# Attention scores as one product of 128 rows per head, with the rope addition split into two halves on GpSimd

## The chip, the cores and the metric

The kernel is one program on one core of a Trainium2 chip. TensorE (PE) multiplies, VectorE (DVE), ScalarE (ACT) and GpSimd (POOL) do the elementwise work, and SyncE (SP) issues the DMAs. The metric is the device time of one execution in microseconds, the lower the better; of several runs the median is given.

## The reference

Two adaLN layers over x of 4 x 512 tokens x 256. The change touches only the attention of the second layer. What it computes there, per batch entry b (4 of them, 512 tokens, 16 query heads, 4 key groups):

```python
qkv = hidden_states @ Wqkv
q, c_kv = jnp.split(qkv, [NH * D_QK], axis=-1)        # c_kv: a latent of 64 per token
q = q.reshape(b, s, NH, D_QK)                         # D_QK = 128 (nope) + 64 (rope)
k = (c_kv @ Wk_up).reshape(b, s, NKV, D_QK)
v = (c_kv @ Wv_up).reshape(b, s, NKV, D_V)
q = jnp.concatenate([q_nope, _rope(q_rope, s)], axis=-1)
k = jnp.concatenate([k_nope, _rope(k_rope, s)], axis=-1)
scores = jnp.einsum('bqhd,bkhd->bhqk', q, k) * scale  # k repeated for 4 heads each
scores = jnp.where(causal[None, None], scores, jnp.finfo(scores.dtype).min)
probs = jax.nn.softmax(scores, axis=-1)
out = jnp.einsum('bhqk,bkhd->bqhd', probs, v).reshape(b, s, NH * D_V)
return out @ Wo
```

`_rope(x)` is `x * cos + rot * sin`, with `rot` the two halves of the 64 rope rows swapped, one of them negated.

## The kernel before

The first layer (a recurrent attention with Newton-Schulz steps, then a feed-forward part) runs up to about 575 us; the second layer's attention runs from 575 to 1018 us; a mixture of experts ends the kernel.

The attention works in the latent space: the nope part of a key is the 64-row latent `ckvT` itself, because the key weights were multiplied into the query weights beforehand (`w_abs`). So a score is a sum over 128 numbers per head: 64 of the query's latent against `ckvT`, and 64 of the roped query against the roped key. Before, they are two products of 64 rows each that add up in one PSUM bank (L2098 and L2101). `q_latent` and `q_rope` hold two heads stacked: head e of a pair in rows 64e to 64e+63. `ckvT` and `keys` hold the same 64 rows twice, so that either head finds them in its own rows. The four products of a pair of heads are a *block*: latent e=0, latent e=1, rope e=0, rope e=1. All are f32, and an f32 product shows in the trace as two weight loads and two passes (MATMUL records), so a block has eight passes.

Work goes in 16 *batches*, each a tile of 128 query rows of one b, in the order q = 1, 3, 0, 2 (`ORDER`), so that the keys seen are 256, 512, 128 and 384 columns wide (causal). I number them n = 0 to 15. A batch has 8 *slots* of a pair of heads each; slot t = 8n + p. In slot t the order written out by hand for each engine is:

- PE: `score(t + 2)`, a block (two slots ahead of the softmax), and then what `Plan` puts into the slot: parts of `weigh(n - 1)` (probabilities by values, products of 32 rows, L2118, at p = 2 and 3, in two parts, or in one where n % 4 is 3), `project_out(n - 1)` (L2132, 8 passes of 256 columns each at p = 6 and 7), `project_q` for the rope rows of the next batch (p = 0, 1) and for its latent rows (p = 4, 5, or 3, 4 where n % 4 is 3), each 16 passes of 128 columns at L2056; the next b's values (L2064) and keys (L2073, a product of 64 rows), and the transposes of a norm (L1591).
- DVE: `largest(t)` (L2454, masks the scores and takes the row maximum, twice), `turn(t - 2)` (L2468, transposes in blocks of 32), `invert(t)` (L2473), and then rotations of queries (L2479) and keys (L2483, L2484), `gate_out`, norms.
- ACT: `exponential(t)` (L2354, twice), `take_out` (L2363), and the copies out of PSUM, `take_rope` (L2342), `take_latent` (L2346), `take_ckv` (L1979), `take_key` (L2334).
- POOL: `add_rope` due for the slot (L2693 multiplies the swapped rows by sin, L2696 adds them to the rows times cos and writes `q_rope`; half 0 and half 1 of the next batch, ahead of `normalize` in slots p = 5 and 6), `add_key` (L2701), `normalize(t)` (L2707), `add_out` (L2714).
- SP: `swap_rope`, `swap_key` (L2779), four DMAs each, and `spread_key` (L2793), four DMAs of 128 KB that write a group's roped key into both row halves of `keys`.

The waits that matter here: `score(t)` waits for the two maxima of slot t - 2, whose banks it takes; at p = 0 and p = 4 it waits for `taken` of the latent half and for `q_roped` of the rope half; at the first batch of a b it waits for `ckv_taken` and for `keys_spread`. `turn(t - 2)` waits for `normalize(t - 2)`. `project_q` waits until ACT has taken what stood in its bank.

Of the kernel before, what the change touches and what calls it, by code (L numbers as in the profile page):

```python
# [1826 lines left out]
def stage_rest(k):  # L1827
# [34 lines left out]
    q_latent, q_rope = (k.wq_switch[:, 2 * NP * P * n:2 * NP * P * (n + 1)].rearrange("p (f n c) -> p f n c", f=2, n=NP) for n in range(2))  # L1862
# [19 lines left out]
    spare = q_rope[:, 0].rearrange("p n c -> p (n c)")  # L1882
    gt, eq = (spare[:, B * E * E * n:B * E * E * (n + 1)].rearrange("p (b e f) -> p b e f", b=B, e=E) for n in range(2))
    bd = [spare[:, 512 + 256 * w:768 + 256 * w].rearrange("p (c b s f) -> p c b s f", c=2, b=B, s=S2) for w in range(2)]
    spare = q_latent[:, 0].rearrange("p n c -> p (n c)")
# [36 lines left out]
    MOVE = 16 * 4  # L1922
# [62 lines left out]
    with nc.Block() as block:  # L1985
        @block.tensor
        def _(pe):
# [93 lines left out]
            def score(t):  # L2081
# [6 lines left out]
                if p % HP == 0:  # L2088
                    wait_taken(pe, "latent", n, p // HP)
                    pe.wait_ge(s["q_roped"], 2 * n + p // HP + 1)  # L2090
                    if n % QT == 0:
                        pe.wait_ge(s["ckv_taken"], 2 * (b + 1))
                        pe.wait_ge(keys_spread[p // HP], MOVE * (b + 1))
                halves = [slice(LORA * e, LORA * e + LORA) for e in range(2)]
                for e, rows in enumerate(halves):
                    if t >= AHEAD:
                        pe.wait_ge(s["maxed"], 2 * (t - AHEAD) + e + 1)
                    nc.tensor.matmul(score_bank[t % AHEAD][e][:, 0:width(n)], q_latent[rows, n % 2, p, :],  # L2098
                                     ckvT[rows, b % 2, 0:width(n)], start=True, stop=False)
                for e, rows in enumerate(halves):  # L2100
                    nc.tensor.matmul(score_bank[t % AHEAD][e][:, 0:width(n)], q_rope[rows, n % 2, p, :],  # L2101
                                     keys[b % 2][rows, p // 2, 0:width(n)], start=False, stop=True).then_inc(s["scored"], 1)
# [214 lines left out]
        def _(act):  # L2317
# [12 lines left out]
            def take_key(b, f):  # L2330
                wait_made(act, "key", b, f)
                if b > 0:
                    act.wait_ge(keys_spread[f], MOVE * b)
                nc.scalar.activation(key_x[b][:, f], filled("key", b, f)[:], ACT.Copy).then_inc(taken_of("key", b, f), 1)  # L2334

            def take_rope(n, half):
                wait_made(act, "rope", n, half)
                if n > 0:
                    act.wait_ge(s["q_roped"], 2 * (n - 1) + half + 1)
# [4 lines left out]
            def take_latent(n, half):  # L2344
                wait_made(act, "latent", n, half)
                nc.scalar.activation(q_latent[:, n % 2, HP * half:HP * half + HP, :].rearrange("p n c -> p (n c)"),  # L2346
                                     filled("latent", n, half)[:], ACT.Copy).then_inc(taken_of("latent", n, half), 1)
# [85 lines left out]
        def _(dve):  # L2433
# [24 lines left out]
            def turn(t):  # L2458
# [6 lines left out]
                if p == 0 and n % QT == 0:  # L2465
                    for f in range(2):
                        dve.wait_ge(keys_spread[f], MOVE * (n // QT + 1))
# [465 lines left out]
```

## Time and profile before

| | |
|---|---|
| median of 3 runs | 1076.84 us (1074.63 to 1078.26) |
| the profiled execution | 1076.94 us |
| its span, first to last instruction | 1075.1 us |
| mean granted TensorE clock | 0.992 of full speed |
| PE busy | 1016.1 us, 95% |
| DVE, ACT, POOL busy | 703.8, 546.1, 433.7 us |
| block products L2098 and L2101, PE busy | 105.8 and 93.5 us (47.5 + 46.0) |
| rope addition L2696 on POOL | 39.2 us in 30, and two more at the start |

The busy time of an engine counts overlapping instructions once. A matmul's record runs until its last result is out, so two passes overlap; what a pass costs PE is read from start to start. In a timeline row the first number is the start, the second the time to the last end, then engine, line, operation, tiles, shape and count; in brackets stands the idle time ahead of it and what ended it.

### The profile page before, as it was taken

Reading aid. Unit: us, or ns where it says so; the run is one execution under the profiler, and the core shown is the slowest. Engines: PE = TensorE matmul, PEld = TensorE weight load, DVE = VectorE, ACT = ScalarE, POOL = GpSimd, SP = SyncE. Lnnn points to the kernel's source line nnn. Section 1 sums busy time; section 2 is a strip of 40 time slices with the busy share of each in tenths; the row PEclk is TensorE's granted clock in tenths of the full one; section 3 lists DMA queues with packets and bytes.
Section 4 is the critical chain, followed back from the end, with each engine's and each line's share of the span. In section 5 each row is a group of like instructions: output and inputs, shape, how many; then the busy total and the mean of one; then the engine's idle time right before and its main releaser. Section 6 shows DMA issues by size and latency. Waiting matters only on the chain.

```text
span 1075.1 us, 25979 instructions
## 1 busy us (share of the span) xinstructions
PE 1016.1 (95%) x10226; PEld 739.7 (69%) x10226; DVE 703.8 (65%) x2121; ACT 546.1 (51%) x1418; POOL 433.7 (40%) x391
## 2 busy tenths in 40 slices
PE   6788999999999999999999999999999999999978
PEld 4567888888878546655667576766767686758646
DVE  4888898898899713122225675747584767667774
ACT  2667777777778531212132543545454545444441
POOL 1222033134145411010106474747475756778610
PEclk9999999999999999999999899999999999999999
DMA  9150000000000009100013011200120003000202
GB/s 322 44 185 2 1 0 0 0 0 0 1 2 2 1 1 294 46 1 1 1 30 70 15 27 31 64 7 21 36 65 22 21 22 79 22 21 22 80 2 80
DMA packets 27887, 44.03 MB, mean 41 GB/s; under 512 B 6928, under 2 KB 16912, under 8 KB 26896
## 3 DMA queue, kind: packets, MB, share of 16 engines
q1 hardware_dynamic: 27792, 42.71, 13.5%
q8 instruction: 66, 1.08, 0.4%
q14 instruction: 29, 0.24, 0.1%
HBM read 21.98 MB, written 2.10 MB: 22 GB/s over the span
## 4 chain that ended last, share of the span: by engine, by line
PE 53%; DVE 5%; ACT 2%; issue 1%; POOL 0%; DVEq 0%
PE quad L2056 10%; PE quad L1705 8%; PE quad L2098 7%; PE quad L2118 7%; PE quad L2101 6%; PE quad L2000 5%; PE quad L2132 5%; PE quad L2196 1%; PE quad L2064 1%; ACT act_probs L2354 1%; PE quad L1591 1%; DVE act_probs L2454 1%; ACT act_probs L2363 1%; PE quad L2019 1%; DVE x_pairs L2484 1%
## 5 line engine op out<-in xcount | busy, mean ns | idle before, releaser
L2707 POOL TENSOR_TENSOR act_probs<-act_probs,rden 128x512 f32<-128x512 f32 (+3 forms) x128 | 171.0, 1339 | 155.7 <-DVE rden L2473 155.6
L2354 ACT ACTIVATE act_probs<-act_probs,neg_max 128x256 f32<-128x256 f32 (+3 forms) x256 | 140.8, 552 | 82.9 <-DVE neg_max L2454 82.6
L2056 PEld LDWEIGHTS quad<-hT,ug_queries 128*128 128x128 f32 x1024 | 120.5, 194 | 30.6 <-issue 18.6
L2056 PE MATMUL quad<-hT,ug_queries 128*128 128x128 f32 x1024 | 132.2, 283 | 3.0 <-ACT act_probs L2363 2.2
L2454 DVE CUSTOM_DVE_ANT_0 act_probs<-quad,mask 128x256 f32<-128x256 f32 (+3 forms) x256 | 115.1, 486 | 6.8 <-PE quad L2101 6.1
L1705 PE MATMUL quad<-hT,ug_raw_switch 128*128 128x512 f32 x256 | 115.8, 602 | 0.0
L2098 PE MATMUL quad<-ckvT,ug_raw_switch 64*128 64x512 f32 (+3 forms) x512 | 105.8, 480 | 6.9 <-DVE neg_max L2454 6.9
L2473 DVE RECIPROCAL rden<-den 128x2 f32<-128x2 f32 x128 | 20.6, 161 | 120.2 <-ACT act_probs L2354 120.1
L1720 DVE SCALAR_TENSOR_TENSOR act_probs<-quad,ws_up,silu_keys 128x512 f32<-128x512 f32 x32 | 24.0, 750 | 102.4 <-ACT silu_keys L1715 102.4
L1705 PEld LDWEIGHTS quad<-hT,ug_raw_switch 128*128 128x128 f32 x256 | 48.0, 192 | 55.7 <-issue 55.5
L1715 ACT ACTIVATE silu_keys<-quad,ws_gate 128x512 f32<-128x512 f32 x32 | 22.0, 687 | 120.5 <-PE quad L1705 120.5
L2468 DVE STREAM_TRANSPOSE wq_wo<-act_probs 128x1024 f32<-128x1024 f32 (+1 forms) x64 | 70.8, 1106 | 3.1 <-POOL act_probs L2707 3.1
L2098 PEld LDWEIGHTS quad<-ckvT,ug_raw_switch 64*128 64x128 f32 x512 | 41.7, 186 | 39.8 <-issue 20.6
L2132 PE MATMUL quad<-down_keys,act_probs 128*128 128x256 f32 x256 | 63.5, 392 | 0.8 <-ACT act_probs L2363 0.8
L1426 POOL TENSOR_TENSOR hidden<-gate_silu,hb 128x256 f32<-128x256 f32 x16 | 12.0, 753 | 124.5 <-ACT hb L969 124.5
L2132 PEld LDWEIGHTS quad<-down_keys,act_probs 128*128 128x128 f32 x256 | 46.1, 189 | 19.2 <-issue 11.4
L2000 PE MATMUL quad<-down_raw_out,act_probs 128*128 128x256 f32 x256 | 56.1, 379 | 2.0 <-PEq L1510 2.0
L2000 PEld LDWEIGHTS quad<-down_raw_out,act_probs 128*128 128x128 f32 x256 | 48.4, 190 | 10.1 <-issue 3.7
L2118 PE MATMUL quad<-wq_wo,latent_rows 32*64 32x256 f32 x1792 | 53.0, 378 | 2.4 <-DVE ug_raw_switch L2500 1.6
L1206 DVE SCALAR_TENSOR_TENSOR q_bf<-quad,silu_keys 128x512 bf16<-128x512 f32 x72 | 46.2, 683 | 5.3 <-PE quad L645 5.1
L2354 ACT ACTIVATION_READ_ACCUMULATOR act_probs<-act_probs,neg_max 128x1 f32 x256 | 48.3, 189 | 0.0
L2118 PEld LDWEIGHTS quad<-wq_wo,latent_rows 32*64 32x64 f32 x1792 | 41.0, 131 | 10.3 <-issue 3.6
(332 smaller groups left out, 2317.6 us busy)
## 6 DMA issues: line engine op xcount, KB each, us to landing
rope_swapped<-gate SPq DMA_DIRECT2D x120, 64.0 KB, 2.0
ug_raw_switch<-in_wmod SPq DMA_DIRECT2D x4, 512.0 KB, 6.3
x_pairs<-in_x SPq DMA_DIRECT2D x4, 512.0 KB, 7.0
x_rows<-x_pairs SPq DMA_DIRECT2D x8, 256.0 KB, 5.0
wq_wo<-in_wq_nopeT SPq DMA_DIRECT2D x1, 2048.0 KB, 8.6
wq_wo<-in_wo SPq DMA_DIRECT2D x1, 2048.0 KB, 12.8
down_raw_out<-x_pairs SPq DMA_DIRECT2D x16, 128.0 KB, 2.3
ug_queries<-in_switch_w SPq DMA_DIRECT2D x1, 2048.0 KB, 7.6
```

The costliest lines, as they stand in the source:

```text
L1206: nc.vector.scalar_tensor_tensor(q_bf[:, q, :], bank[q][:], ca_b2, a_bf[:, q, :], ALU.mult, ALU.add).then_inc(taken[q], 1)
L1705: mm = k.nc.tensor.matmul(k.bank[2 * (m % 2) + w][:], self.w_ug[:, w, kt, P * m:P * m + P], k.hT[:, kt, 2 * i:2 * i + 2, 4 * C * u:4 * C * ...
L2000: mm = nc.tensor.matmul(bank[4 + q // 2][:, D * (q % 2):D * (q % 2) + D], act_t[:, m, P * q:P * q + P], w_down[:, ffn.place(m), :], start= ...
L2056: mm = nc.tensor.matmul(out[:, P * i:P * i + P], w[:, kt, HP * half + i, :], k.hT[:, kt, b, cols], start=(kt == 0), stop=(kt == KT - 1))
L2098: nc.tensor.matmul(score_bank[t % AHEAD][e][:, 0:width(n)], q_latent[rows, n % 2, p, :], ckvT[rows, b % 2, 0:width(n)], start=True, stop=F ...
L2101: nc.tensor.matmul(score_bank[t % AHEAD][e][:, 0:width(n)], q_rope[rows, n % 2, p, :], keys[b % 2][rows, p // 2, 0:width(n)], start=False, ...
L2118: mm = nc.tensor.matmul(av[LORA * e:LORA * e + LORA, i, :], val[rows, b % 2, j, :], src[rows, j, e, :, :], start=(j == 0), stop=(j == bloc ...
L2132: mm = nc.tensor.matmul(out[:, 0:D], oT[:, p, :], w_vo[:, p, :], start=(p == 0), stop=(p == NP - 1))
L2354: nc.scalar.activation(tile, tile, ACT.Exp, bias=neg_max[:, r, e:e + 1], scale=-1.0, accum_out=den[:, r, e:e + 1])\
L2454: nc.vector.tensor_tensor_reduce(probs[:, t % RING, e, 0:cols], score_bank[t % AHEAD][e][:, 0:cols], mask[:, L - cols:L], -QK_SCALE, 3e38, ...
L2468: nc.vector.transpose(turned_of[batches[n][1]][:, :, :, p, :].rearrange("p j e c -> p e j c"), probs[:, t % RING, :, 0:width(n)].rearrange ...
L2707: nc.gpsimd.tensor_tensor(tile, tile, rden[:, t % RING, :].unsqueeze(2).to_broadcast([P, 2, cols]), ALU.mult)\
```

## The change

`q_latent` and `q_rope` become one buffer `query`, with the latent of a head in rows 0 to 63 and its roped rows in rows 64 to 127; `keys` holds the latent in rows 0 to 63 and the roped key in rows 64 to 127, for each of the 4 groups. A block becomes two products of 128 rows (four passes), one per head. ACT copies a latent half in two instructions of 64 rows; POOL adds a rope half in two instructions of 64 rows, each followed by a wait for its own end. SP writes a key once instead of twice, and a new DMA `spread_latents` copies `ckvT` into rows 0 to 63 of `keys` for all 4 groups (512 KB), once per b.

```diff
-    q_latent, q_rope = (k.wq_switch[:, 2 * NP * P * n:2 * NP * P * (n + 1)].rearrange("p (f n c) -> p f n c", f=2, n=NP) for n in range(2))
+    query = k.wq_switch[:].rearrange("p (f e n c) -> p f e n c", f=2, e=2, n=NP)
...
-    MOVE = 16 * 4
+    MOVE, KEY_MOVE = 16 * 4, (16 * 3, 16 * 2)
...
                 if p % HP == 0:
                     wait_taken(pe, "latent", n, p // HP)
-                    pe.wait_ge(s["q_roped"], 2 * n + p // HP + 1)
+                    pe.wait_ge(s["q_roped"], 4 * n + 2 * (p // HP) + 2)
                     if n % QT == 0:
-                        pe.wait_ge(s["ckv_taken"], 2 * (b + 1))
-                        pe.wait_ge(keys_spread[p // HP], MOVE * (b + 1))
-                halves = [slice(LORA * e, LORA * e + LORA) for e in range(2)]
-                for e, rows in enumerate(halves):
+                        for f in range(p // HP + 1):
+                            pe.wait_ge(keys_spread[f], KEY_MOVE[f] * (b + 1))
+                for e in range(2):
                     if t >= AHEAD:
                         pe.wait_ge(s["maxed"], 2 * (t - AHEAD) + e + 1)
-                    nc.tensor.matmul(score_bank[t % AHEAD][e][:, 0:width(n)], q_latent[rows, n % 2, p, :],
-                                     ckvT[rows, b % 2, 0:width(n)], start=True, stop=False)
-                for e, rows in enumerate(halves):
-                    nc.tensor.matmul(score_bank[t % AHEAD][e][:, 0:width(n)], q_rope[rows, n % 2, p, :],
-                                     keys[b % 2][rows, p // 2, 0:width(n)], start=False, stop=True).then_inc(s["scored"], 1)
+                    nc.tensor.matmul(score_bank[t % AHEAD][e][:, 0:width(n)], query[:, n % 2, e, p, :],
+                                     keys[b % 2][:, p // 2, 0:width(n)], start=True, stop=True).then_inc(s["scored"], 1)
...
             def take_latent(n, half):
                 wait_made(act, "latent", n, half)
-                nc.scalar.activation(q_latent[:, n % 2, HP * half:HP * half + HP, :].rearrange("p n c -> p (n c)"),
-                                     filled("latent", n, half)[:], ACT.Copy).then_inc(taken_of("latent", n, half), 1)
+                for e in range(2):
+                    op = nc.scalar.activation(query[0:LORA, n % 2, e, HP * half:HP * half + HP, :].rearrange("p n c -> p (n c)"),
+                                              filled("latent", n, half)[LORA * e:LORA * e + LORA, :], ACT.Copy)
+                op.then_inc(taken_of("latent", n, half), 1)
...
                 pool.wait_ge(s["rope_swept"], 2 * n + half + 1)
                 pool.wait_ge(s["rope_turned"], 2 * n + half + 1)
-                nc.gpsimd.tensor_tensor(q_rope[:, n % 2, HP * half:HP * half + HP, :].rearrange("p n c -> p (n c)"),
-                                        rope_x[n][:, half], rope_w[:, half], ALU.add).then_inc(s["q_roped"], 1)
+                for e in range(2):
+                    rows = slice(LORA * e, LORA * e + LORA)
+                    nc.gpsimd.tensor_tensor(query[LORA:P, n % 2, e, HP * half:HP * half + HP, :].rearrange("p n c -> p (n c)"),
+                                            rope_x[n][rows, half], rope_w[rows, half], ALU.add).then_inc(s["q_roped"], 1)
+                    pool.wait_ge(s["q_roped"], 4 * n + 2 * half + e + 1)
...
             def spread_key(b, f):
                 sp.wait_ge(s["keys_roped"], 2 * b + f + 1)
                 for g in range(2):
-                    for e in range(2):
-                        sp.dma_start(keys[b % 2][LORA * e:LORA * e + LORA, 2 * f + g, :], key_x[b][LORA * g:LORA * g + LORA, f])\
-                            .then_inc(keys_spread[f], 16)
+                    sp.dma_start(keys[b % 2][LORA:P, 2 * f + g, :], key_x[b][LORA * g:LORA * g + LORA, f]).then_inc(keys_spread[f], 16)
+
+            def spread_latents(b):
+                sp.wait_ge(s["ckv_taken"], 2 * (b + 1))
+                sp.dma_start(keys[b % 2][0:LORA], ckvT[0:LORA, b % 2, :].unsqueeze(1).to_broadcast([LORA, NKV, L])).then_inc(keys_spread[0], 16)
...
             for f in range(2):
                 spread_key(0, f)
+                if f == 0:
+                    spread_latents(0)
             for t in range(SLOTS):
                 for _, n, half in due(t, 1, "rope"):
                     swap_rope(n, half)
+                for _, b, half in due(t, 2, "value"):
+                    if half == 1:
+                        spread_latents(b)
```

The other lines of the diff only follow the new names and counts.

## Rows read from the trace of the kernel before

**Rows 1.** Engines over the attention: stretch, length, busy us (instructions), clock.

```profile
575.00:1018.00 443.00, 432.50 (x4669) 306.73 (x4669) 296.59 (x890) 211.39 (x607) 284.64 (x225) 0.99 0.14 35
```

**Rows 2.** Waits over the attention: us in total, times, longest us.

```profile
PE quad L2098 <- DVE neg_max L2454: 6.9, 6, 2.8
```

**Rows 3.** Timeline of PE, n = 3 (384 columns), around the key product.

```profile
655.08 0.92 PE L2098 MATMUL quad<-ckvT,ug_raw_switch 64*128 64x384 f32 x4
...
656.57 1.99 PE L2132 MATMUL quad<-down_keys,act_probs 128*128 128x256 f32 x8
658.50 1.13 PE L2073 MATMUL quad<-ckvT,wk_rope 64*128 64x512 f32 x4
659.46 0.81 PE L2098 MATMUL quad<-ckvT,ug_raw_switch 64*128 64x384 f32 x4
...
660.85 1.99 PE L2132 MATMUL quad<-down_keys,act_probs 128*128 128x256 f32 x8
662.68 1.34 PE L1591 MATMUL quad<-eye,norm_xn 128*128 128x128 f32 x8
```

**Rows 4.** Timeline of PE, long runs of 128-row passes ahead of the attention.

```profile
542.28 10.46 PE L1705 MATMUL quad<-hT,ug_raw_switch 128*128 128x512 f32 x24
...
554.31 7.41 PE L2056 MATMUL quad<-hT,ug_queries 128*128 128x128 f32 x64 [0.51 <-DVE act_probs L1720]
...
561.56 13.98 PE L2000 MATMUL quad<-down_raw_out,act_probs 128*128 128x256 f32 x64
```

**Rows 5.** Timeline of PE, n = 1 (512 columns), two blocks and a projection.

```profile
610.74 1.13 PE L2098 MATMUL quad<-ckvT,ug_raw_switch 64*128 64x512 f32 x4
...
612.66 2.05 PE L2056 MATMUL quad<-hT,ug_queries 128*128 128x128 f32 x16
614.64 1.13 PE L2098 MATMUL quad<-ckvT,ug_raw_switch 64*128 64x512 f32 x4
```

**Rows 6.** Groups by line: weight loads of L2056, then POOL and ACT operations of the change.

```profile
L2056 PEld LDWEIGHTS quad<-hT,ug_queries 128*128 128x128 f32 x1024 | 120.5, 194 | 30.6 <-issue 18.6
L2696 POOL TENSOR_TENSOR ug_raw_switch<-gate,rope_swapped 128x512 f32<-128x512 f32 x30 | 39.2, 1305 | 2.4
L2346 ACT ACTIVATE ug_raw_switch<-quad 128x512 f32<-128x512 f32 x32 | 19.1, 596 | 45.6 <-PE quad L2056 45.6
L1979 ACT ACTIVATE ckvT<-quad 32x512 f32<-32x512 f32 x16 | 9.4, 588 | 18.8 <-PE quad L2064 17.1 <-PE quad L2033 1.6
```

**Rows 7.** Timeline of n = 3: DVE's key rotations and the block behind them.

```profile
666.72 1.96 DVE L2484 TENSOR_TENSOR x_pairs<-x_pairs,rope_sin 128x512 f32<-128x512 f32 x1
...
672.11 0.97 PE L2098 MATMUL quad<-ckvT,ug_raw_switch 64*128 64x384 f32 x3 [1.15 <-DVE neg_max L2454]
```

**Rows 8.** Timeline, end of n = 3: POOL's queue, PE's and DVE's instructions that depend on it.

```profile
678.56 1.83 POOL L2707 TENSOR_TENSOR act_probs<-act_probs,rden 128x768 f32<-128x768 f32 x1 [1.45 <-DVE rden L2473]
...
681.71 1.60 POOL L2696 TENSOR_TENSOR ug_raw_switch<-gate,rope_swapped 128x512 f32<-128x512 f32 x1
...
683.28 1.46 POOL L2707 TENSOR_TENSOR act_probs<-act_probs,rden 128x768 f32<-128x768 f32 x1
...
684.23 0.60 PE L2098 MATMUL quad<-ckvT,ug_raw_switch 64*128 64x256 f32 x4
...
687.28 3.89 POOL L2707 TENSOR_TENSOR act_probs<-act_probs,rden 128x768 f32<-128x768 f32 x3
...
688.78 0.98 DVE L2468 STREAM_TRANSPOSE wq_wo<-act_probs 128x768 f32<-128x768 f32 x1 [1.05 <-POOL act_probs L2707]
```

**Rows 9.** Timeline of PE, n = 2: the first projection behind a weigh.

```profile
650.47 2.05 PE L2056 MATMUL quad<-hT,ug_queries 128*128 128x128 f32 x16 [0.54 <-ACT act_probs L2363]
```

**Rows 10.** Timeline, start of the attention: SP's key DMAs and PE's first block.

```profile
565.83 5.21 SPq L2793 DMA_DIRECT2D silu_keys<-wq_wo  x8
...
575.47 0.70 PE L2098 MATMUL quad<-ckvT,ug_raw_switch 64*128 64x256 f32 x4
```

**Rows 11.** DMA issues of 512 KB: count, KB each, median us from issue to landing.

```profile
x_pairs<-in_x SPq DMA_DIRECT2D x4, 512.0 KB, 7.0
```

More of the change, by code:

```diff
@@ L1881, in stage_rest @@
     w3, b3, parity, before, diagonal = (k.moe[n] for n in ("w3", "b3", "parity", "before", "diagonal"))
-    spare = q_rope[:, 0].rearrange("p n c -> p (n c)")
+    spare = query[:, 0, 0].rearrange("p n c -> p (n c)")
     gt, eq = (spare[:, B * E * E * n:B * E * E * (n + 1)].rearrange("p (b e f) -> p b e f", b=B, e=E) for n in range(2))
     bd = [spare[:, 512 + 256 * w:768 + 256 * w].rearrange("p (c b s f) -> p c b s f", c=2, b=B, s=S2) for w in range(2)]
-    spare = q_latent[:, 0].rearrange("p n c -> p (n c)")
+    spare = query[:, 0, 1].rearrange("p n c -> p (n c)")
     masked = [spare[:, E * BLK * n:E * BLK * (n + 1)].rearrange("p (e r) -> p e r", e=E) for n in range(2)]
@@ L2332, in take_key @@
                 if b > 0:
-                    act.wait_ge(keys_spread[f], MOVE * b)
+                    act.wait_ge(keys_spread[f], KEY_MOVE[f] * b)
                 nc.scalar.activation(key_x[b][:, f], filled("key", b, f)[:], ACT.Copy).then_inc(taken_of("key", b, f), 1)
@@ L2338, in take_rope @@
                 if n > 0:
-                    act.wait_ge(s["q_roped"], 2 * (n - 1) + half + 1)
+                    act.wait_ge(s["q_roped"], 4 * (n - 1) + 2 * half + 2)
                 if n == 1:
@@ L2466, in turn @@
                     for f in range(2):
-                        dve.wait_ge(keys_spread[f], MOVE * (n // QT + 1))
+                        dve.wait_ge(keys_spread[f], KEY_MOVE[f] * (n // QT + 1))
                 nc.vector.transpose(turned_of[batches[n][1]][:, :, :, p, :].rearrange("p j e c -> p e j c"),
```

## The prediction

> **What bounds the kernel now.** I read the busy time by stage first: over the attention, 443 us long, PE is busy for 432.5, DVE for 296.6, ACT for 211.4 and POOL for 284.6, at a granted clock of 0.99 [rows 1]. Next the waits of the same stretch: PE's products idle for the row maxima only six times, 6.9 us in all [rows 2]. So PE's own passes set the pace, and what matters is what they cost beyond streaming columns. That is read in the timeline, from start to start.
>
> In a long run of 128-row passes one costs (7.41 - 0.28) / 63 = 0.113 us at 128 columns and (13.98 - 0.38) / 63 = 0.216 us at 256 (0.28 and 0.38 us are what the last pass's own record lasts) [rows 4]. Weight loads of 0.194 us [rows 6] don't show in that: they run behind the passes. Around a block it is otherwise. The 8 passes at 656.57, between a block and the key product, both of 64 rows, take 1.93 us until 658.50; the 8 at 660.85, a block before and another 128-row product behind, take 1.83; streaming alone is 8 x 0.216 = 1.73 [rows 3]. So going from 128 rows to 64 costs some 0.10, and coming back another 0.10 in the first pass. A block shows the same two halves: 1.49 us between 128-row neighbours (655.08 to 656.57), 1.39 with the 64-row key product ahead (659.46 to 660.85) [rows 3]. I call each meeting of a block with a 128-row product a *side*. A block and a filler with two sides each: the block of 512 columns takes 1.92 us, the filler of 16 passes 1.98 [rows 5]; the filler alone would be 16 x 0.113 = 1.81, and four passes of 512 columns at (10.46 - 0.60) / 23 = 0.429 [rows 4] are 1.71. Excess 0.17 + 0.21 = 0.38 for two sides, and 0.10 + 0.10 from [rows 3] for one; I take **0.195 us a side**, half of it ahead of the border and half behind. No idle time stands in these rows, so a semaphore isn't the cause.
>
> **What the change removes on PE.** The block streams the same columns as before: 8 passes of 64 rows that ran two at a time become 4 of 128 rows, one at a time. What goes is the side. 128 blocks have 256 sides; 26 weigh parts (32 rows) take 52, which stay changes of row count; 3 meet the key product; 19 meet another block or the end (first and last batch mainly, where slots have no filler). 182 are left, counted through the trace. 182 x 0.195 = **35.5 us** if PE sets the pace everywhere.
>
> **What of it is lost, place by place.**
>
> (a) Keys, n = 3, 7, 11. DVE rotates keys, one L2484 taking 1.96 us beside POOL's work; PE then waits 1.15 us for a maximum (672.11) [rows 7]. That chain starts when PE ends the norm transposes begun at 662.68 [rows 3]; the five sides between lie in PE's waiting time: 5 x 0.195 = 0.97 lost each.
>
> (b) POOL's second addition, same batches. One rope addition takes 1.305 us for 128x512 [rows 6]. No POOL row has fewer partitions. Bounds: half (0.65) if time went with partitions; 1.60, the slow one at 681.71 [rows 8]. ACT's copy of 32 partitions takes 0.588 against 0.596 for 128 [rows 6], so I take the full 1.3 for each half, plus 0.1 for each wait for its own end: 1.5 us more per rope half, 30 halves in the attention. The Trainium skill (GPSIMD Engine Reference, section 2.1) says that each of its cores serves its own 16 partitions; no run here shows that yet. Behind the additions stand `normalize` and through it `turn`, `invert` and the next maxima on DVE. In most batches POOL idles between normalizations long enough. At the end of n = 3 it doesn't: normalize ends at 680.4, rope, normalize at 683.28, rope, and three in a row from 687.28, with DVE waiting 1.05 us at 688.78 [rows 8]. PE's first block of the next batch starts at 684.23, 0.9 after the addition at 681.71 ended [rows 8]. With four sides gone ahead of it PE comes 0.8 earlier and the addition ends 1.5 later: PE waits 1.4, and all 0.8 is lost and 0.6 more. DVE's turn is then 3 us later; six more sides, 1.2, are eaten before PE is past its effect, and some 0.5 of the 0.6 stays. Together 0.97 + 0.8 + 1.2 + 0.5 = 3.4, three times: **10.3 us**.
>
> (c) First projection behind a weigh: PE waits there for ACT's take_out, 0.54 us at n = 2 [rows 9], less in the 256-column batches. That side gives nothing, in eight batches: **1.6 us**.
>
> (d) First and last batch: DVE's norm work sets the pace, three of the six waits of [rows 2] stand there. About 20 sides: **3.9 us**. For the additions on POOL in n = 13 and 14, which carry b3, w3 and bias additions too, I take **1.0**, an estimate of two half-hidden delays of the size in (b).
>
> Sum: 35.5 - 10.3 - 1.6 - 3.9 - 1.0 = **18.7 us** off.
>
> **Edits costed at nothing.** ACT's latent copy becomes two of 0.596, so 0.6 more, 32 times. ACT idled 45.6 us ahead of these 32 for PE [rows 6], 1.4 each, and is busy for 211 of 443 [rows 1]; behind it wait the exponentials and, at p = 0, the block. If that cover went it would be 32 x 0.6 = 19 us. The latent DMA: at the start eight key DMAs are issued in 5.21 us from 565.83, so 0.65 each; the new one is third, issued by 567.8 if the key is ready as before; 512 KB landed in 7.0 us [rows 11]: 574.8, against PE's first block at 575.47 [rows 10]. Tight, but the four DMAs of 7.0 shared their engines. If it took 3 more, PE would wait 2 us once. Later it goes at slot 9 of each b, behind half 0's swap and ahead of half 1's; ACT has taken the latent by then, and the swap is wanted three slots of 3.9 us later (1.92 + 1.98, [rows 5]). Fewer key DMAs save only SP's time. A gain that I don't count: head e = 0 is complete after half a block, so DVE starts its maximum up to 0.85 us earlier at 512 columns, which eases every chain behind it, POOL's too.
>
> **The sum.** The profiled execution took 1076.94, 0.1 from the median. 1076.9 - 18.7 = **1058.2**.
>
> **Rivals.**
>
> *Nearly all arrives* (0.12). POOL's halves take 0.65, or the earlier maximum absorbs (b)'s second part: lost are (a), (c), half of (d), so 2.9 + 1.6 + 2.0 = 6.5, and 29 us come off: 1048. For it: DVE and POOL have 33% and 36% idle. Against it: [rows 8] leaves POOL no gap.
>
> *Much is swallowed* (0.15). Compressed slots make stalls like that of [rows 8] in the 512-column batches and in n = 13 and 14 as well, 1 to 2 us for each of seven: 1065 to 1072.
>
> *Same* (0.06). The softmax loop of DVE, ACT and DVE again takes PE's place in every batch; 1074 to 1080. Against it: three engines with 67% or less.
>
> *POOL becomes the bound: slower* (0.05). If each of the 15 batches handed POOL's whole extra 3.0 us to PE, 45 us would come on against 35.5 off: 1086. It decides from 2.4 us per batch on. For it: three batches come near. Against it: in the others POOL waits for DVE before almost every normalization.
>
> *Weight loads come into the open: slower* (0.02). If a load can't run behind a pass of the same rows, each of the four passes of a block pays 0.194: 128 x 4 x 0.194 = 99 us, less 35.5: 1141. Against it: [rows 4], 64 passes of equal rows at 0.113 with such loads. The Trainium skill (TensorE: Matmul & The Clock Gate, part 3, "What overlaps and what doesn't") says that loads overlap running products only where the row group differs; by it this change would lose. The rows disagree with it for full-height products.
>
> **Chances and range.** My forecast, 1050 to 1065, has 0.60. 1048 to 1070 takes in the first rival's value and most of the second's, and leaves out under 0.2. POOL's half at 1.60 instead of 1.3 would cost 3 x 1.2 = 3.6 more (1062); at 0.65 it gives back up to 6 (1052). Three runs differ by 0.3%, so 3.2 us is what can be told: faster 0.87, same 0.06, slower 0.07.
>
> **What would show it.** Passes: filler of 16 between blocks 1.81, block of 512 columns 1.71 to 1.72, of 384 1.29; a slot with L2056 at 512 columns 3.50 to 3.52 in place of 3.90. Borders with weigh unchanged. POOL: two additions of 1.3 for each half. PE waiting for POOL's addition at the first block of n = 4, 8, 12; DVE waiting some 3 us for POOL soon after; the wait of 1.15 at n = 3 grown to about 2.1. I am wrong if the first pass of a filler still takes 0.1 more though both sides have 128 rows, if a half addition is far from 1.3 us, or if DVE waits for POOL in other batches too.

## The result and the profile after

The changed kernel takes 1070.85 us, median of 13 runs (1069.86 to 1073.54), beside 1076.01 (13 runs, 1073.46 to 1079.22) of the kernel before on the same chip: ratio 0.9953, 95% interval 0.9942 to 0.9964. It is faster, by 5 us where 18.7 were forecast, and lies 0.85 above the range. The profiled execution took 1071.87, its span 1070.1, against 1076.94 and 1075.1.

The engines over the attention, in the changed kernel, same stretch and columns as [rows 1]:

```profile
575.00:1018.00 443.00, 412.39 (x4267) 312.98 (x4265) 310.93 (x906) 233.92 (x647) 327.06 (x260) 0.98 0.14 35
```

PE, once busy for all but 10.5 us, now has 30.6 us without a pass (29.7 of them between its first block and its last), and POOL is busy for 327.1, 42.4 more. The waits of the attention (568 to 1010) say for whom PE stands; the columns are total us, times, longest us:

```profile
PE quad L2097 <- DVE neg_max L2452: 19.4, 14, 4.3
DVE wq_wo L2466 <- POOL act_probs L2708: 16.7, 7, 3.4
PE quad L2097 <- POOL ug_raw_switch L2696: 3.4, 3, 1.1
```

The wait for maxima went from 6.9 us, six times [rows 2], to 19.4, fourteen times. DVE's turning (L2466) waits 16.7 us for POOL's normalizations, where it waited 3.1 us, three times, in the kernel before:

```profile
DVE wq_wo L2468 <- POOL act_probs L2707: 3.1, 3, 1.1
```

That DVE waits for POOL in other batches than n = 3, 7 and 11 is one of the signs of being wrong that the prediction named.

The sides are gone as forecast. PE's timeline at n = 1, which answers to [rows 5]:

```profile
610.82 1.88 PE L2097 MATMUL quad<-silu_keys,ug_raw_switch 128*128 128x512 f32 x4
612.53 1.95 PE L2056 MATMUL quad<-hT,ug_queries 128*128 128x128 f32 x16
614.32 1.88 PE L2097 MATMUL quad<-silu_keys,ug_raw_switch 128*128 128x512 f32 x4
```

From start to start the block takes 1.71, the filler 1.79 and the slot 3.50, against 3.90. The addition's group:

```profile
L2696 POOL TENSOR_TENSOR ug_raw_switch<-gate,rope_swapped 64x512 f32<-64x512 f32 x60 | 77.3, 1289 | 4.7
```

Half the partitions cost 1.289 us, against 1.305 for all 128 [rows 6]. (The Trainium skill, GPSIMD Engine Reference, section 2.1, with 16 partitions to each core, agrees.)

Where the time went is seen batch by batch. Worked out from the timelines: us from the first block of a batch to the first block of the next (the last one to its last block), with the columns of its blocks. The tail runs from the start of the last block to the end of the span. The last two columns are kernels of the experiments below.

| n | columns | before | after | one addition | placed, five batches |
|---|---|---|---|---|---|
| 0 | 256 | 22.7 | 22.4 | 20.5 | 20.4 |
| 1, 5, 9, 13 | 512 | 31.9, 34.4, 34.4, 30.9 | 29.5, 32.0, 32.0, 28.6 | 29.4, 32.0, 32.0, 28.6 | 29.4, 32.0, 32.0, 28.6 |
| 2, 6, 10, 14 | 128 | 25.0, 25.1, 25.1, 25.3 | 26.5, 26.6, 25.7, 27.2 | 23.5, 23.5, 23.7, 24.5 | 23.5, 23.6, 23.7, 24.4 |
| 3, 7, 11 | 384 | 29.2, 29.2, 29.2 | 29.3, 29.4, 29.4 | 30.0, 30.0, 30.0 | 30.6, 29.4, 29.4 |
| 4, 8, 12 | 256 | 25.9, 25.9, 25.9 | 24.8, 24.8, 24.9 | 23.9, 24.0, 24.0 | 24.8, 24.9, 24.9 |
| 15 | 384 | 21.5 | 19.7 | 19.7 | 19.7 |
| tail | | 58.1 | 60.3 | 59.8 | 61.8 |

Each 512-column batch gave 2.3 or 2.4, twelve sides' worth. The 128-column batches should have given some 2 each, and took 5.5 more together. That difference of some 13.5 us is as large as the whole miss; how much of it belongs to POOL the experiments tell.

What happens there is in POOL's queue at the end of n = 1. The kernel before:

```profile
621.72 1.27 POOL L2693 TENSOR_TENSOR rope_swapped<-rope_swapped,rope_sin 128x512 f32<-128x512 f32 x1
623.07 1.27 POOL L2696 TENSOR_TENSOR ug_raw_switch<-gate,rope_swapped 128x512 f32<-128x512 f32 x1
625.18 2.26 POOL L2707 TENSOR_TENSOR act_probs<-act_probs,rden 128x1024 f32<-128x1024 f32 x1 [0.84 <-DVE rden L2473]
...
632.48 2.46 POOL L2707 TENSOR_TENSOR act_probs<-act_probs,rden 128x1024 f32<-128x1024 f32 x2 [0.60 <-DVE rden L2473]
```

and the changed kernel, with what follows on DVE and PE:

```profile
621.49 1.27 POOL L2691 TENSOR_TENSOR rope_swapped<-rope_swapped,rope_sin 128x512 f32<-128x512 f32 x1
622.84 2.61 POOL L2696 TENSOR_TENSOR ug_raw_switch<-gate,rope_swapped 64x512 f32<-64x512 f32 x2
625.53 2.22 POOL L2708 TENSOR_TENSOR act_probs<-act_probs,rden 128x1024 f32<-128x1024 f32 x1
627.71 1.27 POOL L2691 TENSOR_TENSOR rope_swapped<-rope_swapped,rope_sin 128x512 f32<-128x512 f32 x1
629.06 2.62 POOL L2696 TENSOR_TENSOR ug_raw_switch<-gate,rope_swapped 64x512 f32<-64x512 f32 x2
631.76 4.32 POOL L2708 TENSOR_TENSOR act_probs<-act_probs,rden 128x1024 f32<-128x1024 f32 x3
...
633.69 1.25 DVE L2466 STREAM_TRANSPOSE wq_wo<-act_probs 128x1024 f32<-128x1024 f32 x1 [1.24 <-POOL act_probs L2708]
...
636.84 1.38 DVE L1566 BATCH_NORM_STATS2 norm_stats<-x_rows 128x6 f32<-128x256 f32 x4
...
639.10 0.87 PE L2097 MATMUL quad<-silu_keys,ug_raw_switch 128*128 128x128 f32 x4 [1.04 <-DVE neg_max L2452]
640.54 5.39 PE L2114 MATMUL quad<-wq_wo,latent_rows 32*64 32x256 f32 x128 [0.57 <-issue]
...
646.50 3.71 PE L2114 MATMUL quad<-wq_wo,latent_rows 32*64 32x256 f32 x128
```

A slot with a rope half asks POOL for 1.27 + 1.27 + 2.26 = 4.8 us in the kernel before, against a slot of 3.90; the queue barely recovers. Now it asks for 1.27 + 2.61 + 2.22 = 6.1 against 3.50, twice in a row, and POOL has no gap from 621.5 to 636.1. Normalizations are late, DVE turns late, DVE's sums for a norm (L1566) come behind that, and the maxima of short blocks come last: PE waits 1.04 for one. PE stands still for 0.57 more ahead of the weigh part, for which the profile names no releaser. The weigh part takes 5.39 us instead of 3.71. The clock in the windows around it (columns as in [rows 1]):

```profile
640.50:646.00 5.50, 5.46 (x129) 4.52 (x130) 4.75 (x14) 1.70 (x8) 4.87 (x6) 0.69 0.23 52
646.50:650.00 3.50, 3.50 (x129) 2.85 (x128) 2.33 (x7) 0.00 (x0) 1.32 (x2) 1.00 0.02 5
```

A mean of 0.69 means that for 3.4 of the 5.5 us the granted clock was 1.2 GHz; behind them it is 2.4. Before the fall PE had waited 1.04 and 0.57.

### The profile page after: what moved, and what is told of

It is laid out like the page before. It is cut to its first block, busy times and chain, and to the rows that moved or that the text cites. A ratio compares the mean times of both kernels' runs of the same rounds, so it can differ in the third digit from the quotient of the medians.

```text
span 1070.1 us, 25039 instructions
## 1 busy us (share of the span) xinstructions
PE 990.9 (93%) x9714; PEld 742.7 (69%) x9714; DVE 712.3 (67%) x2121; ACT 566.3 (53%) x1450; POOL 473.7 (44%) x423
## 4 chain that ended last, share of the span: by engine, by line
PE 38%; POOL 8%; DVE 8%; issue 5%; ACT 4%; POOLq 0%; DVEq 0%
PE quad L1705 8%; PE quad L2114 6%; PE quad L2097 6%; PE quad L2056 5%; PE quad L2000 5%; POOL ug_raw_switch L2696 3%; POOL act_probs L2708 2%; PE quad L2128 2%; ACT act_probs L2352 2%; POOL rope_swapped L2691 2%; DVE act_probs L2452 1%; PE quad L2192 1%; DVE wq_wo L2466 1%; ACT act_probs L2361 1%; PE quad L2064 1%
## 5 line engine op out<-in xcount | busy, mean ns | idle before, releaser
L2708 POOL TENSOR_TENSOR act_probs<-act_probs,rden 128x512 f32<-128x512 f32 (+3 forms) x128 | 168.8, 1325 | 108.0 <-DVE rden L2471 106.2
L2056 PEld LDWEIGHTS quad<-hT,ug_queries 128*128 128x128 f32 x1024 | 124.0, 194 | 17.6 <-issue 6.7
L2056 PE MATMUL quad<-hT,ug_queries 128*128 128x128 f32 x1024 | 126.7, 278 | 3.0 <-ACT act_probs L2361 2.2
L2097 PE MATMUL quad<-silu_keys,ug_raw_switch 128*128 128x256 f32 (+3 forms) x256 | 83.0, 448 | 12.6 <-DVE neg_max L2452 11.5
L2097 PE MATMUL quad<-down_raw_out,ug_raw_switch 128*128 128x256 f32 (+3 forms) x256 | 81.8, 443 | 10.2 <-DVE neg_max L2452 7.9
L2471 DVE RECIPROCAL rden<-den 128x2 f32<-128x2 f32 x128 | 20.5, 160 | 103.9 <-ACT act_probs L2352 103.6
L2466 DVE STREAM_TRANSPOSE wq_wo<-act_probs 128x1024 f32<-128x1024 f32 (+1 forms) x64 | 70.8, 1106 | 16.7 <-POOL act_probs L2708 16.7
L2696 POOL TENSOR_TENSOR ug_raw_switch<-gate,rope_swapped 64x512 f32<-64x512 f32 x60 | 77.3, 1289 | 4.7
L2097 PEld LDWEIGHTS quad<-silu_keys,ug_raw_switch 128*128 128x128 f32 x256 | 42.6, 193 | 36.4 <-issue 20.1
L2097 PEld LDWEIGHTS quad<-down_raw_out,ug_raw_switch 128*128 128x128 f32 x256 | 42.3, 190 | 33.8 <-issue 20.6
L2114 PE MATMUL quad<-wq_wo,latent_rows 32*64 32x256 f32 x1792 | 58.2, 403 | 5.9 <-DVE ug_raw_switch L2498 2.8
L2128 PE MATMUL quad<-down_keys,act_probs 128*128 128x256 f32 x256 | 60.5, 380 | 0.8 <-ACT act_probs L2361 0.8
```

The source lines that it names most:

```text
L2056: mm = nc.tensor.matmul(out[:, P * i:P * i + P], w[:, kt, HP * half + i, :], k.hT[:, kt, b, cols], start=(kt == 0), stop=(kt == KT - 1))
L2097: nc.tensor.matmul(score_bank[t % AHEAD][e][:, 0:width(n)], query[:, n % 2, e, p, :], keys[b % 2][:, p // 2, 0:width(n)], start=True, stop ...
L2114: mm = nc.tensor.matmul(av[LORA * e:LORA * e + LORA, i, :], val[rows, b % 2, j, :], src[rows, j, e, :, :], start=(j == 0), stop=(j == bloc ...
L2128: mm = nc.tensor.matmul(out[:, 0:D], oT[:, p, :], w_vo[:, p, :], start=(p == 0), stop=(p == NP - 1))
L2466: nc.vector.transpose(turned_of[batches[n][1]][:, :, :, p, :].rearrange("p j e c -> p e j c"), probs[:, t % RING, :, 0:width(n)].rearrange ...
L2696: nc.gpsimd.tensor_tensor(query[LORA:P, n % 2, e, HP * half:HP * half + HP, :].rearrange("p n c -> p (n c)"), rope_x[n][rows, half], rope_ ...
```

## The experiments

Two theories at first. P: POOL's second addition swallows the gain. N: what swallows it is DVE's norm work, which stands in the same batches n = 2, 6, 10 and 14. The batch times that follow are from the profiles. Intervals are of the ratio to the kernel before, run on the same chip; its median was 1075.2 beside the first four kernels and 1077.2 to 1077.9 on another chip beside the rest, so differences in us between kernels of different rounds are good to 2 or 3 us.

**One addition.** The changed kernel without the rope rows of head e = 0:

```
-                for e in range(2):
+                for e in (1,):
                     rows = slice(LORA * e, LORA * e + LORA)
                     nc.gpsimd.tensor_tensor(query[LORA:P, ...
```

> The changed kernel, but POOL adds only head e = 1 of each rope half (64 of the 128 rows; the roped rows of head e = 0 are left out). POOL's cost per half is then that of the kernel before, PE's and ACT's that of the changed one. Theory P (POOL's second addition makes normalize late, DVE's turn waits for it, and the maxima and PE behind it): the batches of 128 columns give some 2 us each again in place of losing 1.4, and the wait at the first block of n = 4, 8, 12 goes: 4 x 3.4 + 3 x 2, so 15 to 20 us under the changed kernel, 1051 to 1056. Theory N (DVE's own work, the norm sums above all, sets the pace in those batches once PE is faster): only the n = 4, 8, 12 part comes back, 1063 to 1066.

1057.30 us (4 runs), 0.9825 [0.9805, 0.9844]. The 13.6 us are back, without any change to PE, DVE or ACT. In the profile DVE waits for POOL 2.3 us, four times. The end of n = 1:

```profile
624.25 1.27 POOL L2691 TENSOR_TENSOR rope_swapped<-rope_swapped,rope_sin 128x512 f32<-128x512 f32 x1
625.60 1.26 POOL L2696 TENSOR_TENSOR ug_raw_switch<-gate,rope_swapped 64x512 f32<-64x512 f32 x1
626.94 1.89 POOL L2708 TENSOR_TENSOR act_probs<-act_probs,rden 128x1024 f32<-128x1024 f32 x1
629.34 2.46 POOL L2708 TENSOR_TENSOR act_probs<-act_probs,rden 128x1024 f32<-128x1024 f32 x2 [0.51 <-DVE rden L2471]
```

POOL waits for DVE again. PE's wait of 1.04 is gone, the 0.57 ahead of the weigh part isn't, and the same 128 passes stay at 2.4 GHz:

```profile
636.49 3.71 PE L2114 MATMUL quad<-wq_wo,latent_rows 32*64 32x256 f32 x128 [0.57 <-issue]
```

Of the 14.7 us between the two profiled spans, 10.8 lie in n = 2, 6, 10 and 14, and 1.9 in n = 0. The granted clock doesn't explain it: worked out from windows of 2 us, both profiles have 13.6 us at 1.2 GHz within the attention (the kernel before has 6.8), only in other batches: here 3.4 less in n = 0, none in n = 2 and 6, and 3.4 each in n = 3, 7 and 11.

The time lies 1.3 above the range of P. The forecast without its POOL terms is 1049.8 (worked out in the expectation of one addition and one copy, below), so 7.5 us of it are missing even without the second addition.

**The kernel before with the addition in two.** Same engine order, blocks of 64 rows:

```
+                for e in range(2):
+                    rows = slice(LORA * e, LORA * e + LORA)
+                    nc.gpsimd.tensor_tensor(q_rope[rows, ...], rope_x[n][rows, half], rope_w[rows, half], ALU.add)...
```

> The kernel before, with nothing but POOL's addition split into two of 64 rows with a wait behind each, each head written to its own old rows. PE is as slow as before. Theory P: POOL's backlog costs here too, less since PE leaves more time: 3 to 6 us slower than before, 1079 to 1082, with DVE waiting for POOL at the end of the 512- and 384-column batches. Theory N: under 1 us.

1082.12 (4 runs), 1.0055 [1.0035, 1.0074]: the second addition alone costs 0.55%, 5.9 us, with 64-row blocks, and 1.3%, 13.6 us, with 128-row ones. In the profile the batches n = 2, 6 and 10 take what they take in the kernel before, within 0.2; n = 3, 7 and 11 take 0.5 more each and n = 14 takes 1.6 more. The two parts don't add up: each side that PE loses makes POOL's slot shorter.

**The sin multiplication two slots earlier** (changed kernel, both additions):

```
+                for _, n, half in due(t, 3, "rope"):
+                    sweep_rope(n, half)
                 for _, n, half in due(t, 5, "rope"):
                     add_rope(n, half)
```

> The changed kernel with POOL's multiplication by sin moved two slots ahead of the additions (slots p = 3 and 4 in place of 5 and 6); a wait for POOL's last instruction stands in front of the additions. POOL does as much work, but spread: 2.6 us in slots 5 and 6 in place of 3.9. Theory P: most of POOL's cost goes, 8 to 14 us under the changed kernel, 1057 to 1063. Theory N: 1067 to 1070.

1063.55 (4 runs, 1061.87 to 1067.64), 0.9876 [0.9854, 0.9898]. POOL's work is the same, only spread over four slots in place of two, and half the loss is gone, just short of what P expected: at least half is the bunching, not the total. n = 2, 6, 10 and 14 took 25.2, 27.3, 24.8, 28.1, in the slowest of the four runs.

**The norms moved to n = 1, 5, 9 and 13:**

```
-norms = {0: 6, 2: 7, 6: 8, 10: 9, 14: 10}
+norms = {0: 6, 1: 7, 5: 8, 9: 9, 13: 10}
```

> The changed kernel with four norms (sums, normalization, transposes) moved one batch ahead, out of the 128-column batches n = 2, 6, 10, 14 into the 512-column batches n = 1, 5, 9, 13; nothing else. Theory P: POOL's backlog at the end of the 512-column batches stays, 0 to 3 us under the changed kernel. Theory N: the stalls of n = 2, 6, 10, 14 go with the two clock windows behind them, 8 to 14 us under the changed kernel, 1057 to 1063.

1081.89 (5 runs), 1.0052 [1.0035, 1.0070], worse by 11 us than the changed kernel, which neither theory expected. n = 6 and 10 do fall to 24.0, but n = 5 and 9 rise from 32.0 to 37.9. In DVE's timeline of n = 5:

```profile
735.04 5.94 DVE L1584 TENSOR_SCALAR norm_xn<-x_rows,norm_mv,norm_rstd 128x256 f32<-128x256 f32 x4
```

and in PE's, behind the maximum that follows it:

```profile
741.64 3.00 PE L2097 MATMUL quad<-down_raw_out,ug_raw_switch 128*128 128x512 f32 x4 [2.12 <-DVE neg_max L2452]
```

So the norm work does cost in the 128-column batches, once maxima are late, but DVE has less room in the others. As the cause by itself N is out: with one addition the norms stay where they are and the loss goes.

**One addition and one copy.** Also without ACT's copy of the latent of head e = 0 (query rows 0 to 63):

> The changed kernel with POOL adding, and ACT copying, for head e = 1 of each pair only (the query rows of head e = 0 are left out; PE, DVE and every other step as in the changed kernel). The same with both copies and one addition took 1057.3. If ACT's second copy of 0.6 us is hidden, as the prediction had it, this gives 1056.5 to 1058. If the copy costs something where PE waits for take_out behind a weigh part, 0.3 to 0.6 us in each of 15 batches come off: 1049 to 1053. Sum of the prediction without its POOL terms: the forecast of 1058.2 less 3.4 x 3 without the 3 x 0.97 of the keys' sides, less 1.0, so 1049.8; a value well above 1053 says that some of the sides are lost on DVE and ACT, not on POOL.

1053.32 (4 runs, 1051.62 to 1054.87), 0.9776 [0.9737, 0.9815]. Between the profiles only n = 3, 7 and 11 differ by more than 0.1 (30.0 each against 29.4, 28.1, 28.1), and the tail, 2.6 longer here. n = 7 in the kernel with one addition and both copies:

```profile
775.96 2.21 PE L2097 MATMUL quad<-down_raw_out,ug_raw_switch 128*128 128x384 f32 x4 [1.94 <-DVE neg_max L2452]
778.10 2.92 PE L2114 MATMUL quad<-x_pairs,latent_rows 32*64 32x256 f32 x64
```

and with one addition and one copy:

```profile
774.97 1.53 PE L2097 MATMUL quad<-down_raw_out,ug_raw_switch 128*128 128x384 f32 x4 [1.95 <-DVE neg_max L2452]
776.85 1.99 PE L2114 MATMUL quad<-x_pairs,latent_rows 32*64 32x256 f32 x64 [0.35 <-issue]
```

The wait is the same; in one run the passes behind it go at half clock. So in n = 7 and 11 the copy doesn't make PE wait; a stretch at 1.2 GHz (3.4 us long, so 1.7 us of passes) makes most of the 1.9 us. The time lies between the two ranges expected, the two intervals meet, and why the medians lie 4.0 apart isn't wholly explained.

**One copy, both additions:**

> The changed kernel, both additions, with ACT copying the latent of head e = 1 only (the latents of head e = 0 stay those of another batch or none). The prediction costed the second copy of 0.6 us, 32 times, at nothing. Hidden: 1068 to 1071. Between one addition with both copies (1057.3) and with one copy (1053.3) lay 4 us; if that was the copy and not a matter of half clock stretches, 3 to 5 us come off here too: 1066 to 1068.

1070.30 (6 runs), 0.9939 [0.9917, 0.9960], beside 0.9953 [0.9942, 0.9964]. The copy costs nothing that can be told, as the prediction had it.

**The sin multiplication on DVE** (changed kernel, POOL keeps the two additions):

```
+                nc.vector.tensor_tensor(w, w, sin[:, cols].unsqueeze(1).to_broadcast([P, HP, P]), ALU.mult)...
```

> The changed kernel with the sin multiplication (L2691, 1.27 us on POOL) done by DVE right behind its cos multiplication, so that POOL has the two additions alone for each rope half, 2.6 us as in the kernel before, and DVE 0.7 to 2.0 us more. If POOL's queue in slots 5 and 6 of the 512-column batches is what swallowed the gain (theory P), the waits of DVE for POOL's normalize in n = 2, 6, 10, 14 go and the time is 1058 to 1064, less good than one addition (1057.3) because DVE is loaded instead. If DVE's row of the same slots is what is full (rival D: DVE's own work sets the maxima), it moves the load to the wrong engine: 1071 to 1078.

1072.70 (10 runs), 0.9960 [0.9943, 0.9977]. The 128-column batches fall to 24.1, 24.2, 24.2, 25.6: POOL's queue was their trouble. But n = 3, 7 and 11 rise to 31.2, 32.8, 31.4 and n = 8 to 26.8, and PE waits 22.5 us for maxima in all: the time is that of the rival, DVE. Not all of it need be DVE's load. In n = 7 and 8 stand 10.2 us at half clock too, and POOL's additions now wait for the multiplication:

```profile
POOL ug_raw_switch L2700 <- DVE rope_swapped L2479: 19.1, 28, 0.7
```

So P holds in the 128-column batches; for the others the experiment shows that DVE has no room for the multiplication, not which of the three costs how much.

**One addition, then two DMAs that place the halves:**

```
+            def place_rope(n, half):
+                sp.wait_ge(s["q_roped"], 2 * n + half + 1)
+                for e in range(2):
+                    sp.dma_start(query[LORA:P, n % 2, e, ...], rope_x[n][LORA * e:LORA * e + LORA, half])...
```

> The changed kernel with one 128x512 addition on POOL for each rope half, written in place as before, and two DMAs of SP, 128 KB each, that put the two heads' rows under the latents. Everything of the function is computed. Theory P: POOL has the load of the kernel before, so the time is that of one addition (1057.3) plus what the transfers' landing of some 2.5 to 4 us costs at the first block of the batches that wait for the addition already: 0 to 2 us in each of n = 4, 8, 12, so 1057 to 1063. Rival: the second addition isn't the cause, or the transfer comes too late for the first block of every batch: 1068 or more.

1063.40 (4 runs, 1060.68 to 1066.24), 0.9870 [0.9825, 0.9915]. n = 2, 6, 10 and 14 take 23.5, 23.5, 23.7, 24.4, what one addition gave. But n = 3, 7 and 11 take 31.8, 30.8 and 31.8 against 30.0, and n = 12 takes 25.5 against 24.0. Part of the price stands at the first block of n = 4:

```profile
682.62 1.10 PE L2098 MATMUL quad<-down_raw_out,ug_raw_switch 128*128 128x256 f32 x4 [2.32 <-DMA ug_raw_switch<-gate]
```

**The same with the early sin multiplication:**

> The one before (one addition, two DMAs) with the sin multiplication brought forward by two slots, to slots 3 and 4. Moving it alone in the changed kernel gave 1063.6 against 1070.9. Theory P: with half of POOL's rope work out of slots 5 and 6 normalize(14) and (15) come earlier still and the transfers start up to 1.3 us earlier: 1054 to 1058, up to 3 us below the kernel without it. If POOL's queue is no longer what anything waits for, it is the same within 1 us.

1059.50 (4 runs), 0.9844 [0.9804, 0.9884]: 3.9 us less than without the early multiplication, though the intervals overlap and it lies 1.5 above the range.

**DMAs for n = 1, 2, 6, 10 and 14 alone,** two additions elsewhere:

```
+    PLACED = (1, 2, 6, 10, 14)
...
+                if n in PLACED:
+                    nc.gpsimd.tensor_tensor(rope_x[n][:, half], rope_x[n][:, half], rope_w[:, half], ALU.add)...
+                    return
```

> The changed kernel with only the rope rows of n = 1, 2, 6, 10 and 14 put in place by one addition and two DMAs for each half; all else, the place of the sin multiplication too, as in the changed kernel. If the second additions queued in slots 5 and 6 ahead of n = 2, 6, 10, 14 are what swallowed the forecast gain, and those elsewhere cost little, this alone returns most of it: the four batches go from 26.5, 26.6, 25.7, 27.2 us to some 23.5 to 24.4, 11 us, n = 0 from 22.4 to 20.5, 2 us: 1056 to 1061. If the loss is spread over all batches, one third of the 13.6 us between the changed kernel and that with one addition: 1065 to 1068.

1060.99 (5 runs), 0.9853 [0.9830, 0.9876]: one addition taken from POOL in five of fifteen batches returns 10 of the 13.6 us (last column of the table: n = 2, 6, 10 and 14 give 10.8, n = 0 gives 2.0; n = 3, with a stretch at half clock, and the tail, with 6.8 us of it for 3.4, take 2.8 back). This places the loss that the second addition causes. The 2.0 of n = 0 is mostly clock: in every profile of 128-row blocks n = 0 takes 20.4 or 20.5 where it has 3.4 us at half clock, and 22.1 to 23.0 where it has 6.8.

**That, with the early sin multiplication:**

> Everything computed. The sin multiplication two slots earlier; the rope rows of n = 1, 2, 6, 10 and 14 put under the latents by one addition and two DMAs for each half, those of the other ten batches by the two additions on POOL. With the transfers everywhere (1059.5) the batches n = 3, 7, 11 took 31.0, 30.5, 29.6 us, against 30.1, 28.6, 28.6 with the additions (the first block of the next batch waits for the transfer there, 2.9 us once); with the additions everywhere (1063.6) n = 2, 6, 10, 14 took 25.2, 27.3, 24.8, 28.1, against 23.5, 23.6, 23.7, 23.8. Theory P, the cost is local to POOL's queue ahead of the 128-column batches: the better of the two in each place, 1059.5 less 0.9 + 1.9 + 1.0, so 1054 to 1058. Rival, the two interact (split additions in n = 3, 4, 7, 8 make later batches late again): 1059 to 1064.

1056.96 (5 runs, 1055.75 to 1057.15), 0.9815 [0.9792, 0.9838]. It computes everything, beats both kernels, and is 1.2 us from the time that the prediction gave the change, by chance: the forecast had charged 8.4 us for the second additions, most of which this kernel doesn't pay. PE's waits:

```profile
PE quad L2108 <- DVE neg_max L2463: 11.1, 6, 4.1
```

n = 0 takes 22.2 there, against 20.4 without the early multiplication; the early multiplication from n = 1 on was not tried.

**The kernel before with the early sin multiplication:**

> The kernel before with its sin multiplication two slots earlier. There PE's passes set the pace and the maxima are late six times only, so by theory P bringing POOL's work forward gives nothing: within 0.3% of the kernel before, 0 to 3 us off. If the early multiplication is worth something whatever the blocks' height (rival), it takes the 7.3 us off that it takes off the changed kernel: ratio 0.993.

1074.31 (12 runs), 0.9975 [0.9960, 0.9991]. That is 0.25%, small but beyond the interval's doubt. Batch by batch n = 1 to 14 are the same within 0.3 us; only n = 0 differs, 19.0 for 22.7, where the kernel before has 6.8 us at half clock from 591.7 and this profile none. So POOL's bunching costs nothing in n = 1 to 14 as long as PE is slow. The 7.3 us in the changed kernel belong to the change.

Taking away POOL's waits for its own additions was not tried. They are small in any case: two additions of 1.27 with their waits take 2.61.

## Why the prediction was wrong

**What held.** The price of a side (0.195) and its place: the slot went from 3.90 to 3.50, blocks take 1.71 and fillers 1.79, and the 512-column batches gave 2.3 to 2.4. The weight loads stay behind full-height passes: 1024 loads of L2056 at 194 ns, and a filler of 16 passes still at 0.112 each. (The Trainium skill, TensorE: Matmul & The Clock Gate, part 3, "What overlaps and what doesn't", lets loads overlap only across row groups; by that sentence this kernel would have lost, and it gained.) The half addition costs the full 1.3. ACT's second copy is hidden. The start of n = 4 is close to [rows 8] as foreseen:

```profile
684.77 1.10 PE L2097 MATMUL quad<-down_raw_out,ug_raw_switch 128*128 128x256 f32 x4 [1.13 <-POOL ug_raw_switch L2696]
...
691.72 0.98 DVE L2466 STREAM_TRANSPOSE wq_wo<-act_probs 128x768 f32<-128x768 f32 x1 [3.38 <-POOL act_probs L2708]
```

1.13 for 1.4 forecast, 3.38 for "some 3", and the wait of [rows 7] went from 1.15 to 1.94 for 2.1 forecast. n = 3 and 4 together gave 1.0, where their 23 sides (4.5) less the 3.4 of (a) and (b) are 1.1.

**The step that failed** is in (b): "In most batches POOL idles between normalizations long enough." It had the mechanism, and looked for it in one place. (b) was charged three times, at n = 3, 7 and 11, where the trace of before already shows DVE waiting for POOL. It holds four more times, at the end of n = 1, 5, 9 and 13, where that trace shows no wait, only gaps of 0.84 and 0.6 us in a queue that was given 2.6 us more and 0.8 us less time. The 1.0 for n = 13 and 14 is the only part of it that the sum had. Measured against one addition, n = 2, 6 and 10 lost 3.0, 3.1 and 2.0 (the last without a stretch at half clock; another profile of the same additions has such a stretch in n = 10 too, and 26.6 us instead of 25.7, so that it is worth 0.9), and n = 14 lost 2.7.

Measured by leaving it out, the second addition costs 13.6 us. The sum had 8.4 for it (10.3 less the 3 x 0.97 of (a), and 1.0), so 5 of the 13.5 us missed are the step (b).

**The term that wasn't there.** The other 8 or so are missing with one addition too. Against the kernel before, n = 2, 6, 10 and 14 gave 1.5, 1.6, 1.4 and 0.8 there for some 2 each; n = 3, 7 and 11 took 0.8 more for 1.4 less; start and tail took 2.6 more; n = 0 and 15 gave 4.0 where the sum had nothing. Each of n = 3, 7 and 11 has PE's wait of (a), 1.94 or 1.95, and behind it 3.4 us at half clock, which cost 1.7 us of passes; where the clock held, in two of these batches with one copy, they took 28.1, 1.1 less than the kernel before.

The sum has no term for the clock. Over all runs the kernels with 64-row blocks were granted 0.990 to 0.997, those with 128-row blocks 0.982 to 0.992, the changed kernel 0.989 in the median. Of the kernel before, runs at 0.997 took 1073.3 to 1075.1 us and those at 0.991 1079.9 to 1080.4, so a thousandth is worth about 1 us, and the step from its usual 0.994 to 0.989 an estimated 5 us. That the lower clock comes from PE's additional waits fits the traces (waits for maxima of 6.9 us in the kernel before, 19.4 in the changed one, 12.7 with one addition), but no experiment isolates it, and some stretches lie in code that the change doesn't touch.

**The rivals.** *Much is swallowed* named stalls like that of [rows 8] in the 512-column batches and n = 13 and 14, 1 to 2 us each, 1065 to 1072. It is what happened in kind and time: the queue is that of the 512-column batch, the bill comes in the 128-column batch behind it, and it is 2 to 3 us. Its chance, 0.15, was too low. *POOL becomes the bound* was to decide from 2.4 us per batch on; 13.6 us over fifteen are 0.9.

**Terms around it.** (a) measured 0.8 for 0.97. (d) was too dark: the last batch gave 1.8 and the first 0.3. Against that, the attention began 1.6 us later and the tail took 2.2 more. Both have a stretch at half clock that the profile of before hasn't, the first ahead of the attention in code that the change doesn't touch, the second behind a wait of 2.75 us for DVE (a weigh part of 48 passes takes 2.87 for 1.55). With other kernels the tail lay between 58.5 and 62.4, so neither can be put down to the change by these profiles.

**Left open.** Why the clock falls behind one wait of 1.94 us and not behind another of the same length, in n = 7 of one addition with both copies and with one, was not settled; it moves single batches by 1 to 2 us and so limits what one profile can say. Nor why n = 0 has 6.8 us at half clock with the second addition and 3.4 with one, which makes 1.7 of the 1.9 us that it loses. And whether the changed blocks, by letting PE wait, cause the lower clock of their kernels, or how much of it.

## What to carry to other kernels

Before work is moved to an engine with a third of its time idle, add up its queue slot by slot at the place where the work lands, against the slot's new, shorter length: a rope slot asked POOL for 4.8 us of 3.9 before and 6.1 of 3.5 after, and no wait of DVE in the trace of before showed it. A gain on the bounding engine and a cost on another don't add: the same addition cost 5.9 us under the slow blocks and 13.6 under the fast ones. When a gain goes missing, durations by batch of both traces find the place in one table, and spreading or moving the suspect's work in that place alone proves it. Compare the granted clock of all runs too: a change that makes TensorE faster and lets it wait more can lose part of the gain there, some 5 us here by estimate.

## What the runs showed of the hardware

An addition on 64 partitions costs POOL what it costs on 128 (1.289 and 1.305 us). The same work moved to DVE is dear beside POOL. In the kernel with the sin multiplication on DVE:

```profile
623.62 2.22 POOL L2712 TENSOR_TENSOR act_probs<-act_probs,rden 128x1024 f32<-128x1024 f32 x1
624.02 2.38 DVE L2479 TENSOR_TENSOR rope_swapped<-rope_swapped,rope_sin 128x512 f32<-128x512 f32 x1
```

The multiplication takes 0.68 us at its shortest and 2.38 beside POOL's normalization, which itself takes 2.22 instead of 1.89; the mean of its 32 is 1.68. (The Trainium skill, GPSIMD Engine Reference, section 1, lists the interfaces to SBUF as shared with VectorE, with contention for VectorE instructions that have two SBUF inputs; the multiplication is one.) Two DMAs of 128 KB did the placing that cost POOL 1.3 us, and landed 2.3 us after issue.
